# Attention stage: softmax weights' normalisation moved from VectorE to ScalarE, and ScalarE's order changed

## The reference

```python
q = layernorm(x); k = v = ctx                      # 8 heads; every channel is on its own
corr = ifft(fft(q) * conj(fft(k))).real            # over the 256 times
w, idx = top_k(corr, 11);  w = softmax(w)
out = sum_i w_i * v[min(idx_i + t, 255)]           # a correlation of the sparse w with v
x1  = x + out
```

## Time and profile before

| | |
|---|---|
| median of 3 runs | 3328.31 us (3325.06 to 3330.03) |
| the profiled execution's own time | 3329.48 us |
| its span | 3327.7 us |
| attention stage | from 0 to about 1280 us of the span |
| mean busy shares, 400 to 600 us: PE, DVE, POOL, ACT | 94%, 96%, 91%, 82% |
| granted clock of TensorE, 200 to 1200 us | 1.00 |

### The profile page before, as it was taken

One profiled execution on the slowest core, in us unless ns is written; L12 is line 12 of the kernel. 1 busy time (PEld: TensorE's weight loads), 2 busy tenths in 40 slices (PEclk: granted clock), 3 DMA queues, 4 the chain that ended last, 5 costly groups with the idle time before them and its releaser, 6 DMA issues. The chain is left out here.

```text
span 3327.7 us, 46695 instructions
## 1 busy us (share of the span) xinstructions
PE 2989.0 (90%) x12946; PEld 1599.5 (48%) x12946; DVE 2748.3 (83%) x7148; ACT 2262.8 (68%) x5947; POOL 1588.3 (48%) x1165
## 2 busy tenths in 40 slices
PE   5999999999999997999999999999999999367786
PEld 3666666666666663444444444444444444222222
DVE  4999999999999995667978788796978878568776
ACT  6788888887878753655767667586666746376662
POOL 5898998999989872001112122211212120035665
PEclk8999999999999998999999999999999999578997
DMA  5555555455654435353736447473644645425543
GB/s 195 180 155 173 166 160 176 157 171 170 183 180 155 144 95 166 108 174 100 216 119 174 159 135 213 128 202 112 198 149 150 184 127 128 154 92 205 220 170 153
DMA packets 272038, 532.17 MB, mean 160 GB/s; under 512 B 32664, under 2 KB 132760, under 8 KB 248992
## 3 DMA queue, kind: packets, MB, share of 16 engines
q1 hardware_dynamic: 245600, 422.17, 40.6%
q10 hardware_dynamic: 15168, 71.34, 7.4%
q0 software_dynamic: 11008, 35.66, 3.1%
HBM read 401.07 MB, written 128.02 MB: 159 GB/s over the span
## 5 line engine op out<-in xcount | busy, mean ns | idle before, releaser
L1040 PE MATMUL acc<-xh,wq 128*128 128x512 f16 x4096 | 1204.7, 381 | 47.3 <-DVE x_first L1702 17.4
L1040 PE MATMUL acc<-xl,wq 128*128 128x512 f16 x2048 | 758.3, 380 | 0.0
L1268 ACT ACTIVATE unused<-c_first,minus_guess 128x256 bf16<-128x256 f32 x1024 | 505.2, 494 | 283.2 <-DVE minus_guess L1576 222.6
L1040 PEld LDWEIGHTS acc<-xh,wq 128*128 128x128 f16 x4096 | 400.1, 98 | 532.8 <-DVE x_first L1702 22.6
L969 POOL DMA_DIRECT2D c_first<-ctx_pairs x120 | 66.4, 554 | 865.5 <-DVE mk L1627 855.0
L1040 PEld LDWEIGHTS acc<-xl,wq 128*128 128x128 f16 x2048 | 200.8, 98 | 242.8 <-issue 1.9
L435 PEld LDWEIGHTS bu<-m_iz,zf 128*128 128x128 f32 x2048 | 281.4, 193 | 51.8 <-issue 38.0
L435 PE MATMUL bu<-m_iz,zf 128*128 128x128 f32 (+2 forms) x2048 | 295.8, 303 | 6.5 <-POOL zf L275 6.5
L454 PE MATMUL bx<-m_ic,pf 128*128 128x256 f32 x1024 | 239.8, 388 | 36.8 <-POOL pf L339 36.8
L454 PEld LDWEIGHTS bx<-m_ic,pf 128*128 128x128 f32 x1024 | 191.9, 192 | 72.6 <-POOL pf L339 48.5
L2161 PE MATMUL lw<-x,rt 128*66 128x512 f32 x256 | 142.6, 710 | 71.5 <-DVE x L2373 71.5
(11 more groups left out here) (354 smaller groups left out, 7043.5 us busy)
## 6 DMA issues: line engine op xcount, KB each, us to landing
wq<-w_split SPq DMA_DIRECT2D x512, 256.0 KB, 3.3
c_first<-ctx SPq DMA_DIRECT2D x64, 512.0 KB, 6.6
xt<-xT SPq DMA_DIRECT2D x64, 512.0 KB, 6.3
x_pairs<-xo SPq DMA_DIRECT2D x64, 512.0 KB, 3.3
c_first<-ctx_pairs POOLq DMA_DIRECT2D x128, 256.0 KB, 4.8
x<-xn_pairs SPq DMA_DIRECT2D x32, 1024.0 KB, 6.9
out_pairs<-ost SPq DMA_DIRECT2D x32, 1024.0 KB, 4.8
x_first<-x SPq DMA_DIRECT2D x15, 2048.0 KB, 7.6
```

Source lines behind the costliest of these rows:

```text
L1040: return pe.matmul(acc[b][:], ws[(WQ * o + k // CK) % WR][:, k % CK, a, :], x[:, k, :], start=start, stop=False)
L1268: act.activation(signs[:, u // 2, t] if n == COUNTS - 1 else unused[u % 2][:], ct[k % CR][:, t], ACT.Sign, bias=guess[q % 2][:, u:u + 1], ...
```

## The change

On VectorE the four operations `bu * wrec + xt` become one addition over the whole chunk, `bu + xt` into `xo`, and it is moved behind the fold of the weights. The multiplication by `wrec` is done in place in `bu` by four ACTIVATE(Copy, scale=wrec) on ScalarE, between VectorE's joining and its addition, with a new semaphore `scaled_ok`. On ScalarE the copy `w_back`, the four scalings, both halves of the correlations and the Square now come directly behind the copy of `bu` into `xo`, in this order; mean, squares and `w_rows` come behind them, where they were ahead, and `std` stays last. The semaphore `x1_sum` counts once per chunk instead of four times.

```diff
--- before.py
+++ after.py
@@ -153,6 +153,7 @@
         wn_in = [sem(f"w_rows_in{i}") for i in range(2)]
         w_out = [sem(f"w0_out{i}") for i in range(2)]
         w_scaled, w_hi, w_lo, w_summed, w_sums_out = map(sem, ("w0_scaled", "w0_hi", "w0_lo", "w0_summed", "w0_sums_out"))
+        scaled_ok = sem("scaled_ok")
         sq1_ok, halves_ok, chunk_ok, added_ok = map(sem, ("sq1_ok", "halves_ok", "chunk_ok", "added_ok"))
         N_CONST = 5
         block = stack.enter_context(nc.Block())
@@ -243,7 +244,7 @@
                     kk = k - AFTER_I
                     s, c, bb = kk % 2, kk % CH, kk // CH
                     pair = counted(sp, it + bb // 2)
-                    sp.wait_ge(x1_sum, CT * (h + 1))
+                    sp.wait_ge(x1_sum, h + 1)
                     sp.dma_start(x1[bass.ds(pair, 1), :, c * CT:(c + 1) * CT, bb % 2 * L:(bb % 2 + 1) * L].rearrange("a p j t -> p (a j) t"), xo[s][:]).then_inc(x1_out[s], 16)
                 if it is ITS and k == AFTER_W + 2:
                     sp.wait_ge(w_summed, LAST)
@@ -426,7 +427,7 @@
                 if g is not None:
                     s = (k - AFTER_I) % 2
                     if least(g, 1):
-                        pe.wait_ge(x1_sum, CT * g)
+                        pe.wait_ge(x1_sum, g)
                     for a0, part in ((0, ze_sum), (TT, zo_sum)):
                         pe.wait_ge(part, g + 1)
                         for j in range(CT):
@@ -594,6 +595,25 @@
                         act.wait_ge(x1_out[s], 16 * (4 * it + kk // 2))
                         act.wait_ge(sq1_ok, g - 1)
                     act.activation(xo[s][:, :, 0:P - 1], bu[:].rearrange("p b (h t) -> p (b h) t", h=2)[:, :, 0:P - 1], ACT.Copy).then_inc(odd_sb, 1)
+                if t is not None:
+                    act.wait_ge(t_mm, t + 1)
+                    if least(t, 1):
+                        act.wait_ge(fold_ok, 2 * t)
+                    act.activation(wb[:], by[:, 1, :], ACT.Copy).then_inc(wb_sb, 1)
+                if g is not None:
+                    act.wait_ge(joined_ok, g + 1)
+                    act.wait_ge(w_rec, g + 1)
+                    for j in range(CT):
+                        half = bu[:, j // 2, (j % 2) * L:(j % 2 + 1) * L]
+                        act.activation(half, half, ACT.Copy, scale=wrec[(k - AFTER_I) % 2][:, j:j + 1]).then_inc(scaled_ok, 1)
+                if f is not None and least(f, 2):
+                    act.wait_ge(w_cut, CT * (f - 1))
+                correlations(f, 0)
+                correlations(f, 1)
+                if g is not None:
+                    s = (k - AFTER_I) % 2
+                    act.wait_ge(x1_sum, g + 1)
+                    act.activation(xt[s][:], xo[s][:], ACT.Square).then_inc(sq1_ok, 1)
                 mean(it, k, 0)
                 squares(it, k, 0)
                 h = chunk(it, k, AFTER_W + 1)
@@ -601,23 +621,10 @@
                     w = wn[h % 2]
                     act.wait_ge(wn_in[h % 2], 16 * (h // 2 + 1))
                     act.activation(w[:], w[:], ACT.Copy, scale=W_SCALE, accum_out=wrow[:, h:h + 1]).then_inc(w_summed, 1)
-                if t is not None:
-                    act.wait_ge(t_mm, t + 1)
-                    if least(t, 1):
-                        act.wait_ge(fold_ok, 2 * t)
-                    act.activation(wb[:], by[:, 1, :], ACT.Copy).then_inc(wb_sb, 1)
                 b = batch(it, k - 3)
                 if b is not None:
                     act.wait_ge(ln_mv, b + 1)
                     act.activation(std[:], var[:], ACT.Sqrt, bias=eps[:], scale=1.0 / D).then_inc(ln_std, 1)
-                if f is not None and least(f, 2):
-                    act.wait_ge(w_cut, CT * (f - 1))
-                correlations(f, 0)
-                if g is not None:
-                    s = (k - AFTER_I) % 2
-                    act.wait_ge(x1_sum, CT * (g + 1))
-                    act.activation(xt[s][:], xo[s][:], ACT.Square).then_inc(sq1_ok, 1)
-                correlations(f, 1)
             steps(step)
 
         @block.vector
@@ -697,7 +704,7 @@
                         dve.scalar_tensor_tensor(wk[s][:, j, :], co[s][:, j, :], top[s][:, j, TOPK - 1:TOPK], bz[:, j // 2, (j % 2) * L:(j % 2 + 1) * L], ALU.is_ge, ALU.mult, accum_out=wsum[:, j:j + 1]).then_inc(w_cut, 1)
                     dve.wait_ge(w_cut, CT * (t + 1))
                     if least(t, 2):
-                        dve.wait_ge(x1_sum, CT * (t - 1))
+                        dve.wait_ge(x1_sum, t - 1)
                     dve.reciprocal(wrec[s][:], wsum[:]).then_inc(w_rec, 1)
                 variance(it, k)
                 if g is not None:
@@ -711,13 +718,6 @@
                     dve.wait_ge(apart_ok, g + 1)
                     dve.tensor_tensor(plus, plus, odd, ALU.add).then_inc(joined_ok, 1)
                     dve.wait_ge(joined_ok, g + 1)
-                    dve.wait_ge(xt_in[s], 16 * (4 * it + kk // 2 + 1))
-                    if least(g, 2):
-                        dve.wait_ge(x1_out[s], 16 * (4 * it + kk // 2))
-                        dve.wait_ge(added_ok, g - 1)
-                    dve.wait_ge(w_rec, g + 1)
-                    for j in range(CT):
-                        dve.scalar_tensor_tensor(xo[s][:, j, :], bu[:, j // 2, (j % 2) * L:(j % 2 + 1) * L], wrec[s][:, j:j + 1], xt[s][:, j, :], ALU.mult, ALU.add).then_inc(x1_sum, 1)
                 if t is not None:
                     s = (k - AFTER_T) % 2
                     dve.wait_ge(wb_sb, t + 1)
@@ -725,6 +725,15 @@
                         dve.wait_ge(wo_mm, t)
                     dve.tensor_tensor(we[:, 0, :], by[:, 0, :], wb[:], ALU.add).then_inc(fold_ok, 1)
                     dve.tensor_tensor(we[:, 1, :], by[:, 0, :], wb[:], ALU.subtract).then_inc(fold_ok, 1)
+                if g is not None:
+                    kk = k - AFTER_I
+                    s = kk % 2
+                    dve.wait_ge(xt_in[s], 16 * (4 * it + kk // 2 + 1))
+                    if least(g, 2):
+                        dve.wait_ge(x1_out[s], 16 * (4 * it + kk // 2))
+                        dve.wait_ge(added_ok, g - 1)
+                    dve.wait_ge(scaled_ok, CT * (g + 1))
+                    dve.tensor_tensor(xo[s][:], bu[:].rearrange("p b (h t) -> p (b h) t", h=2), xt[s][:], ALU.add).then_inc(x1_sum, 1)
                 if f is not None:
                     s = (k - AFTER_F) % 2
                     if least(f, 2):
```

## The result

| | before | after |
|---|---|---|
| median | 3329.17 us | 3432.16 us (3428.38 to 3434.08, 4 runs) |
| ratio to before, 95% interval | | 1.0309 (1.0297 to 1.0322) |
| span of the profiled execution | 3327.7 us | 3431.0 us |

The kernel became 103 us slower; 3437 was forecast. Nearly all of it lies in the attention stage: the start of the last products with `kf` (L629 before, L636 after) moved from 1257.1 to 1358.0 us of the span, 101 us. What stands behind took 2070.6 us before and 2073.0 after.

What follows compares the result with a forecast made beforehand. The prediction took a loop through VectorE's products, GpSimd and TensorE as the bound. ScalarE's order and GpSimd's delay, 72 us, plus TensorE's clock, 37, gave 109 us and a median of 3437 us, range 3385 to 3475.

Steps and rivals of the forecast that it cites:

- The loop of 18.77 us: Attention stage: VectorE's products, GpSimd and TensorE set the step at 18.77 us; VectorE's output is not on it.
- A: Attention step after D in the four-step cycle, with the mean on ScalarE: forecast 18.77 us, change 0.
- C: Attention step after B, with `std` and its table load on ScalarE: forecast 21.22 us, +2.45.
- B: Attention step after A, with two squares on ScalarE: forecast 20.78 us, +2.01.
- The scalings, 1.67 us: Four in-place ScalarE scalings ahead of VectorE's addition: 1.67 us, bounds 1.3 to 2.0, costing nothing themselves there.
- ScalarE's order: Square, mean or squares and `w_rows` now stand ahead of `kf`: 9.40 us after A, 10.19 after B, 6.87 after C.
- D: Attention step after C, with a table load ahead of Exp: forecast 19.81 us, +0.49, through GpSimd's later `token_sums`.
- The clock: TensorE's idle time ahead of the transposes slows its clock: 14 falls in C, 7 in B, 1.74 us each, 37 us.
- Rival 1: Attention stage: the chain through ScalarE costs 72 us but TensorE's clock holds: 3400 us, chance 0.24.
- Rival 2: Only GpSimd's delay by the later Square counts, ScalarE's late work is absorbed: 31 us, 3360 us, chance 0.06.
- Rival 3: VectorE is the bound, so the change is faster by 28 us: 3300 us, chance 0.05.
- SyncE's queue: Loads for W's split wait some 6 us later for `w_rows`, other transfers queue behind: costed at 0.

Runs made afterwards that it cites:

- exchange on GpSimd: Kernel before with GpSimd's sums into `pf` moved ahead of the low part of W: 3314.1 us, ratio 0.9953.
- ScalarE's order alone: Kernel before with only ScalarE's new order; VectorE keeps its four output operations, no scaling on ScalarE: 3431.5 us, ratio 1.0301.
- fillers: Changed kernel with three additional TensorE matmuls in each step B and C and one in D, results overwritten: 3397.3 us, ratio 1.0220.
- Square alone: Kernel before with only the Square moved behind the second half of the correlations: 3367.7 us, ratio 1.0118.
- C filled: Changed kernel with three additional TensorE matmuls in each step C, between inverse transform and transposes: 3420.1 us, ratio 1.0270.
- B and C filled: Changed kernel with three additional TensorE matmuls in each step B and each step C: 3420.2 us, ratio 1.0279.
- layer norm alone late: Kernel before with only mean, squares, `w_rows` and `std` moved behind the second half of the correlations: 3372.4 us, ratio 1.0133.

## Why the prediction was right

- **The loop of 18.77 us**: confirmed for A and C by the exchange on GpSimd; B stayed at 18.76 there, as ScalarE's queue (0.37 us of VectorE's waiting for `w_back`) was a second bound just below. VectorE's saving of 0.4 us brought nothing: the run with ScalarE's order alone does not have it and takes the same time.
- **The scalings, 1.67 us**: they took 1.54. VectorE's wait for them was 0.19 us in the step C shown and 0.4 at most, not what sets the step; the run with ScalarE's order alone gives the same time without them.
- **ScalarE's order**: 10.07 us from correlations to `kf` after B where 10.19 was worked out. Without the clock B came to +1.76 (forecast +2.01), C to +2.31 (+2.45), D to +0.60 (+0.49; the forecast's own terms, 41.48 + 3.99, give +0.42), A to 0. The chain is 67 us in the traces, forecast 72; the 2.4 us put on the last two steps are not seen, as the last two were no longer than before.
- **Where the wait would show**: I put it at the cut of the weights. Most of it stands earlier, at L692, where VectorE first needs `kf` (2.60 us), with 0.39 left at the cut, where 2 to 3 were forecast. And D's wait of `kf` is gone altogether; only A keeps 1.51, as forecast.
- **The clock**: 30 us, forecast 37. The cost of a fall was about right: 1.67 us on the matmuls of the correlation (5.29 against 3.62) and 1.7 per cycle (82.0 against 80.3), forecast 1.74. The count was not: 14 in C as forecast, but 2 in B where I gave 7. The idle time in C was 3.45 us; the 3.6 of the forecast does not follow from its walk, which gives 3.34. The Trainium skill (TensorE: Matmul & The Clock Gate, HAM oscillation — how this bites in real kernels) tells of a wait that repeats with every tile and slows the clock each time; these traces agree for the wait in step C (14 falls in 14 cycles), but not for the one in B, which repeated just as often and slowed the clock twice.
- **The total**: both terms were a little too large, 109 us where the traces show 97, and some 6 us of the slowdown lie where neither term looked. That 3437 came within 5 us of 3432 is in part luck.
- **Rival 1** (3400) is the case that the fillers made: 3397. **Rival 2** was the right mechanism for a part: Square alone is 1.35 us per cycle at full clock. **Rival 3** fell twice: VectorE was not the bound, and where it was, the move to ScalarE with the order that came with it cost 60 us. The Trainium skill's advice to optimize the engine of highest occupancy first (Perfetto Trace Analysis, Identifying the Most-Contended Engine) pointed at VectorE, with 96%; GpSimd with 91% and ScalarE with 82% stood in the chains that could be shortened, and doing so brought 38 us (3328.0 to 3290.4).
- **SyncE's queue** at 0: no engine's wait ended by its loads shows in the stage. SyncE itself waited up to 5.9 us for `w_rows` ahead of its loads for W, as worked out, and nobody waited for them.

## What to carry to other kernels

When four engines are all over 80% busy, walk the loop of releasers instead of reading the shares, and note for every in-order queue where its slack lies: work that ran while the queue waited anyway is free there, and costs in full behind the wait. Before moving an operation to a less busy engine, ask what that engine does between the operation's release and the next thing that others need from it. And keep filler work, table loads and bookkeeping in the waits: a one-element Exp and two exchanges of order gained more than the change could have.

## What the runs showed of the hardware that I had not expected

In four kernels with quite different idle times (changed, ScalarE's order alone, C filled, B and C filled) the profiled execution's cycle of four steps came to 82.0 us, with one fall of the clock in it; only the few cycles with a fall in B and in C were longer. Filling one idle time made another one bring the fall: 3.45 us in C, then 2.76 us in B, then 1.55 and 0.71 us with the transposes between them in D.

Whether an idle time slows the clock depends on more than its length, as the same idle times both held and fell:

| idle time of TensorE ahead of the correlation | kernel | falls |
|---|---|---|
| 2.77 us, B | changed | 2 of 14 |
| 2.77 us, B | C filled | 13 of 14 |
| 2.48 us, C | layer norm alone late | 7 of 14 |
| 1.65 and 0.70 us, D | changed | 0 of 14 |
| 1.65 and 0.70 us, D | Square alone late | 10 of 14 |
| 1.55 and 0.70 us, D | C filled | 0 of 14 |
| 1.55 and 0.70 us, D | B and C filled | 14 of 14 |

What chooses the idle time, and why so different kernels end at one length of cycle, is not settled by these runs. What they do show is that a fall made its step 1.4 to 1.7 us longer wherever it came, and that in the filled kernel whose longest idle time was 0.93 us there was none from 100 to 1240 us. That is no limit: the kernel before had 1.65 us in every D and no fall either.
